# Mixture-of-experts tail of a transformer layer: nine full tiles last, added straight into the output

## The reference

```python
xn = layernorm(h)
gates = softmax(xn @ Wg + bg)                 # 8 experts
g = gates * top_2_mask; g = g / sum(|g|)
y_e = gelu(xn @ W1[e] + b1[e]) @ W2[e] + b2[e]   # 256 -> 1024 -> 256
out = h + sum over the token's two experts of g_e * y_e
```

## Time and profile before

| what | value |
|---|---|
| time, median of 3 runs (lowest, highest) | 585.12 us (585.07, 585.44) |
| time of the profiled execution | 583.82 us |
| its span in the profile | 582.0 us |
| PE busy | 521.7 us, 90% of the span |
| DVE, ACT, POOL busy | 235.3, 267.6, 200.6 us |
| mean load of the 16 DMA engines, last two of 40 slices | 1 and 4 tenths |
| bytes moved | 78.55 MB |

### The profile page before, as it was taken

The page is one execution under the profiler, slowest core; times in us unless marked ns, Lnnn a source line. Parts: engine busy times, 40 slices in busy tenths (PEclk is TensorE's granted clock), DMA queues, the critical chain, the costliest instruction groups (busy, mean ns, idle before and its releaser), DMA issues.

```text
span 582.0 us, 13228 instructions
## 1 busy us (share of the span) xinstructions
PE 521.7 (90%) x3742; PEld 427.2 (73%) x3743; DVE 235.3 (40%) x1083; ACT 267.6 (46%) x1003; POOL 200.6 (34%) x186
## 2 busy tenths in 40 slices
PE   4799889899889988986899999999999999999990
PEld 3466555566556655644899989999999999999970
DVE  2677677777658756644112411111111111111110
ACT  1267677778667766844334332333333333333310
POOL 3132133224443344361133355333333333333221
PEclk9899999999889988985999999999999999999995
DMA  8890020212030303037556565666666666666614
GB/s 264 270 294 2 19 92 20 93 36 92 2 91 18 91 19 92 18 102 255 169 150 170 160 173 176 182 181 182 180 181 181 181 180 181 181 181 182 180 25 153
DMA packets 50999, 78.55 MB, mean 135 GB/s; under 512 B 10528, under 2 KB 39472, under 8 KB 50768
## 3 DMA queue, kind: packets, MB, share of 16 engines
q1 hardware_dynamic: 40160, 66.80, 35.5%
q0 software_dynamic: 8592, 10.58, 10.8%
q10 hardware_dynamic: 2208, 0.71, 0.6%
HBM read 68.27 MB, written 11.90 MB: 138 GB/s over the span
## 4 chain that ended last, share of the span: by engine, by line
PE 50%; issue 28%; POOL 9%; DMA 4%; DVE 3%; another core or an unknown queue 2%; ACT 2%; POOLq 0%; SPq 0%; DVEq 0%; ACTq 0%
PE psVO L972 21%; PE psS L960 12%; PE psP L960 11%; POOL kbd L259 4%; DMA fold<-xn_dram,sel 2%; POOL rstd L424 2%; POOL meta_dram L433 2%; PE psQK L790 2%; PE psQK L948 2%; ACT prob L587 1%; DMA sel<-meta_dram 1%; PE psP L823 1%; DVE prob L1138 1%; DMA sum_dram<-fold,sel 1%
## 5 line engine op out<-in xcount | busy, mean ns | idle before, releaser
L972 PE MATMUL psVO<-xw,prob 128*128 x624 | 141.6, 380 | 0.8 <-DVE fold L1359 0.8
L972 PEld LDWEIGHTS psVO<-xw,prob 128*128 128x128 f32 x624 | 115.6, 190 | 15.5 <-issue 1.2
L487 POOL DMA_INDIRECT sum_dram<-fold,sel x39 | 61.7, 1582 | 167.3 <-DMA sel<-meta_dram 123.5
L587 ACT ACTIVATE prob<-prob,smin 128x128 f32<-128x128 f32 x256 | 99.5, 394 | 10.4 <-DVE smin L1138 8.1
L680 ACT ACTIVATE prob<-psS,b1T 128x128 f32<-128x128 f32 x160 | 45.5, 368 | 98.1 <-PE psS L960 93.0
L424 POOL TENSOR_TENSOR rstd<-ve,minus_half 128x1 f32<-128x1 f32 x32 | 29.0, 906 | 165.1 <-DVE ve L1101 165.1
L680 ACT ACTIVATE prob<-psP,b1T 128x128 f32<-128x128 f32 x152 | 43.2, 373 | 85.5 <-PE psP L960 81.6
L960 PEld LDWEIGHTS psS<-fold,w1c 128*128 128x128 f32 x640 | 77.0, 198 | 1.9 <-DVE fold L1354 1.0
L960 PE MATMUL psS<-fold,w1c 128*128 128x128 f32 x640 | 77.6, 281 | 0.6 <-DVE fold L1354 0.6
L960 PEld LDWEIGHTS psP<-fold,w1c 128*128 128x128 f32 x608 | 70.7, 192 | 3.0 <-DVE fold L1354 2.1
L960 PE MATMUL psP<-fold,w1c 128*128 128x128 f32 x608 | 71.1, 275 | 1.9 <-DVE fold L1354 1.9
(11 more groups left out here) (165 smaller groups left out, 542.9 us busy)
## 6 DMA issues: line engine op xcount, KB each, us to landing
w1c<-in_L_ffn_W SPq DMA_DIRECT2D x39, 1024.0 KB
xw<-in_x SPq DMA_DIRECT2D x16, 512.0 KB, 7.2
xw<-in_L_ffn_W SPq DMA_DIRECT2D x8, 1024.0 KB
sum_dram<-h_all SPq DMA_DIRECT2D x17, 128.0 KB
xn_dram<-xn SPq DMA_DIRECT2D x16, 128.0 KB
out<-sum_dram SPq DMA_DIRECT2D x4, 512.0 KB, 5.7
relb<-in_L_ffn_b SPq DMA_DIRECT2D x1, 1024.0 KB, 4.7
sel<-meta_dram SPq DMA_DIRECT2D x39, 2.0 KB
```

What stands on the lines that cost most here:

```text
L487: pool.indirect_dma_start(out=sum_dram.ap()[0:EARLY_B * S if j < EARLY else N_TOK + P, :], out_offset=bass.IndirectOffsetOnAxis(ap=row_no[ ...
L587: i = act.activation(blk, blk, ACT.Exp, bias=smin[:, k:k + 1], scale=-1.0, accum_out=ssum[:, k:k + 1])
L972: i = pe.matmul(psVO[:, 0:D], hT[u][:, c * P:(c + 1) * P], xw2[:, bass.ds(e * (HC * D) + c * D, D)], start=(c == 0), stop=(c == HC - 1))
```

## The change

- The experts' full tiles of all sixteen images are at least 25, so nine more than the sixteen early ones are certainly full (`LAST` = 9). They are worked on last, as tiles 30 to 38. The `MID` = 14 tiles between (16 to 29) hold the rest, among them all tiles that are partly filled or unused.
- When the scatter of tile 29 has landed, SP copies `sum_dram` to `out` by the same four DMAs, between the loads for tile 33 and those for tile 34. POOL waits for these copies (`fin_out`) before the scatter of tile 30, and scatters 30 to 38 add to `out`. The copies at the end are gone.
- POOL's order from tile 33 on is `gather(33)`, `gather(34)`, `scatter(30)`, then `gather(j)`, `scatter(j-4)`. So four scatters instead of three stand behind the last pair of a gather and a scatter.
- `yout` has two buffers. DVE waits for the scatter of tile j-2 to land, and POOL for that of tile j-1 before it issues scatter j.
- The tables are made in three pieces. The late counts come between result 5 and `xs_evac(8)`, the table of the middle tiles between result 6 and `xs_evac(9)`, that of the last tiles between result 7 and `xs_evac(10)`; `tables_ok` then counts to 3. Two operations per table that were not waited for are now.

```diff
-LATE = TILES - EARLY
+LAST = -(-(SLOTS - E * (P - 1)) // P) - EARLY
+MID = TILES - EARLY - LAST
+TABLE = max(EARLY, MID, LAST)
...
-        yout = fold[:, 3 * D:4 * D]
+        yout = [fold[:, 3 * D:4 * D], sel[:, 0:D]]
...
-            sp.wait_ge(tables_ok, 2)
+            sp.wait_ge(tables_ok, 3)
             sp.wait_ge(scat, 16 * TOPK * B)
             next_records(EARLY)
             load_w1(EARLY - 1, 1)
-            with sp.Fori(EARLY // 2, TILES // 2) as t:
+            with sp.Fori(EARLY // 2, (EARLY + MID) // 2 + 2) as t:
+                for u in range(2):
+                    next_records(2 * t + (u + 1))
+                    load_w1(2 * t + u, u)
+            out_v = out.rearrange("b p d -> (b p) d")
+            rows_ = N_TOK // 4
+            sp.wait_ge(y_scat, 16 * (EARLY + MID))
+            for i in range(4):
+                sp.dma_start(out_v[i * rows_:(i + 1) * rows_, :],
+                             sum_dram.ap()[i * rows_:(i + 1) * rows_, :]).then_inc(fin_out, 16)
+            with sp.Fori((EARLY + MID) // 2 + 2, TILES // 2) as t:
                 for u in range(2):
                     next_records(2 * t + (u + 1))
                     load_w1(2 * t + u, u)
             load_w1(TILES - 1, 0)
+            sp.wait_ge(fin_out, 16 * 4)
             sp.wait_ge(y_scat, 16 * TILES)
-            out_v = out.rearrange("b p d -> (b p) d")
-            rows_ = N_TOK // 4
-            for i in range(4):
-                sp.dma_start(out_v[i * rows_:(i + 1) * rows_, :],
-                             sum_dram.ap()[i * rows_:(i + 1) * rows_, :]).then_inc(fin_out, 16)
-            sp.wait_ge(fin_out, 16 * 4)
...
             def scatter(j):
                 pool.wait_ge(y_sb, j + 2)
+                if j > 0:
+                    pool.wait_ge(y_scat, 16 * j)
+                if j == EARLY + MID:
+                    pool.wait_ge(fin_out, 16 * 4)
                 own_wait(pool)
                 pool.indirect_dma_start(
-                    out=sum_dram.ap()[0:EARLY_B * S if j < EARLY else N_TOK + P, :],
+                    out=sum_dram.ap()[0:EARLY_B * S if j < EARLY else N_TOK + P, :] if j < EARLY + MID
+                    else out.rearrange("b p d -> (b p) d"),
                     out_offset=bass.IndirectOffsetOnAxis(ap=row_no[:, j * META + 2:j * META + 3], axis=0),
-                    in_=yout, in_offset=None, compute_op=ALU.add).then_inc(y_scat, 16)
+                    in_=yout[j % 2], in_offset=None, compute_op=ALU.add).then_inc(y_scat, 16)
...
                 gather(j)
-                scatter(j - 3)
+                if j < EARLY + MID + 3:
+                    scatter(j - 3)
+                elif j > EARLY + MID + 3:
+                    scatter(j - 4)
...
-            for j in range(TILES - 3, TILES):
+            for j in range(TILES - 4, TILES):
                 scatter(j)
...
+            def early_tables():
+                tile_counts(c_t[:, :], 0)
+                tile_table(0, EARLY, c_t[:, :])
+                dve.sem_inc(tables_ok, 1)
+            def late_counts():
+                tile_counts(c_t[:, :], 0)
+                then(dve.tensor_tensor(c_t[:, :], c_t[:, :], taken[:, 0:E], ALU.subtract))
+                tile_ends(c_t[:, :])
+                tiles_taken(c_last, c_t[:, :], LAST)
+                then(dve.tensor_tensor(taken_too[:, 0:E], taken[:, 0:E], c_last, ALU.add))
+                tile_counts(c_all, P - 1)
+                then(dve.tensor_tensor(c_all, c_all, taken_too[:, 0:E], ALU.subtract))
+            def middle_table():
+                tile_table(EARLY, MID, c_all, taken_too)
+                dve.sem_inc(tables_ok, 1)
+            def last_table():
+                tile_table(EARLY + MID, LAST, c_last, taken)
+                dve.sem_inc(tables_ok, 1)
...
-                if not (isinstance(j, int) and j == 0):
-                    dve.wait_ge(y_scat, 16 * j)
-                dve.tensor_scalar(yout, ysum, metas[:, bass.ds(j * META + 1, 1)], None, ALU.mult) \
+                if not (isinstance(j, int) and j <= 1):
+                    dve.wait_ge(y_scat, 16 * (j - 1))
+                dve.tensor_scalar(yout[u], ysum, metas[:, bass.ds(j * META + 1, 1)], None, ALU.mult) \
                     .then_inc(y_sb, 1)
```

More of the change, by code:

```diff
@@ L168, in vit_layer_kernel @@
         row_no = metas.bitcast(I32)
[L169 to L173, removed]
+        at = 1280
+        c_ge, c_gt = (fold[0:1, at + i * TABLE * E:at + (i + 1) * TABLE * E] for i in range(2))
+        at += 2 * TABLE * E
+        c_w, incl = (fold[0:1, at + i * E * E:at + (i + 1) * E * E] for i in range(2))
+        at += 2 * E * E
+        c_e, c_off, c_in, tile_no = (fold[0:1, at + i * TABLE:at + (i + 1) * TABLE] for i in range(4))
+        at += 4 * TABLE
+        c_step, c_room, c_all, c_last, taken_step = (fold[0:1, at + i * E:at + (i + 1) * E] for i in range(5))
+        at += 5 * E
+        taken, taken_too = (fold[0:1, at + i * (E + 1):at + (i + 1) * (E + 1)] for i in range(2))
         psS = [ps("psS0"), ps("psS1")]
@@ L1326, in tile_table @@
                 then(dve.tensor_tensor(c_in[:, 0:tiles], tile_no[:, 0:tiles], c_off[:, 0:tiles], ALU.add))
-                if late:
-                    then(dve.tensor_scalar(c_in[:, 0:tiles], c_in[:, 0:tiles], taken[:, 0:1], float(E * ROW_TILES),
+                if first is not None:
+                    then(dve.tensor_scalar(c_in[:, 0:tiles], c_in[:, 0:tiles], first[:, 0:1], float(E * ROW_TILES),
                                            ALU.add, ALU.min))
-                dve.tensor_scalar(tile_row[:, at:at + tiles], c_in[:, 0:tiles], float(P), None, ALU.mult) \
-                    .then_inc(tables_ok, 1)
@@ L1333, in tiles_taken @@
[L1333 to L1338 removed]
+                then(dve.tensor_scalar(tile_row[:, at:at + tiles], c_in[:, 0:tiles], float(P), None, ALU.mult))
@@ new lines, in tiles_taken @@
+            def tiles_taken(dst, src, tiles):
+                then(dve.tensor_tensor(c_room[:, :], src, c_end[:, :], ALU.subtract))
+                then(dve.tensor_scalar(c_room[:, :], c_room[:, :], float(tiles), 0.0, ALU.add, ALU.max))
+                then(dve.tensor_tensor(dst, c_room[:, :], src, ALU.min))
+            def early_tables():
[10 more added lines that the diff above has]
+                then(dve.tensor_tensor(c_all, c_all, taken_too[:, 0:E], ALU.subtract))
@@ L1378, in _ @@
             xs_evac(2)
-            result(0, expert(0))
+            result(0, 0, expert(0))
             xs_evac(3)
-            result(1, expert(1))
+            result(1, 1, expert(1))
             xs_evac(4)
-            result(2, expert(2))
+            result(2, 0, expert(2))
             keep_logits(B - 1)
@@ L1389, in _ @@
             masks(B // NG - 1)
-            result(3, expert(3))
+            result(3, 1, expert(3))
             xs_evac(6)
             gates(B // NG - 1)
-            result(4, expert(4))
+            result(4, 0, expert(4))
             rows(B // NG - 1)
             xs_evac(7)
-            result(5, expert(5))
-            tile_table(EARLY, LATE, P - 1, True)
-            dve.wait_ge(tables_ok, 2)
+            result(5, 1, expert(5))
+            late_counts()
             xs_evac(8)
-            result(6, expert(6))
-            with dve.Fori(8, TILES - 1) as j:
-                xs_evac(j + 1)
-                result(j - 1, expert(j - 1))
-            for j in range(TILES - 2, TILES):
-                result(j, expert(j))
+            result(6, 0, expert(6))
+            middle_table()
+            xs_evac(9)
+            result(7, 1, expert(7))
+            last_table()
+            dve.wait_ge(tables_ok, 3)
+            xs_evac(10)
+            result(8, 0, expert(8))
+            xs_evac(11)
+            with dve.Fori(5, TILES // 2 - 1) as t:
+                for u in range(2):
+                    result(2 * t + (u - 1), 1 - u, expert(2 * t + (u - 1)))
+                    xs_evac(2 * t + (u + 2))
+            result(TILES - 4, 1, expert(TILES - 4))
+            xs_evac(TILES - 1)
+            for j in range(TILES - 3, TILES):
+                result(j, j % 2, expert(j))
 _INS = ['x', 'L0_tok_w1', 'L0_tok_b1', 'L0_tok_w2', 'L0_tok_b2', 'L0_attn_Wq', 'L0_attn_Wk', 'L0_attn_Wv',
```

38 lines of the change are left out of this document (18 added, 20 removed).

## The result

| | before | after |
|---|---|---|
| median of 5 runs (lowest, highest) | 585.44 us (585.07, 586.60) | 582.30 us (581.76, 582.45) |
| profiled execution, its span | 583.82, 582.0 us | 581.76, 580.0 us |

The ratio is 0.9935, with a 95% interval of 0.9908 to 0.9962. The change gains 3.1 us where 8.3 were predicted, and the time lies above the predicted range.

The account below looks back on a forecast made before the run. PE alone was taken to set the pace in the middle of the expert stage, with copies and scatters behind it at the end. Terms: -9.0 - 0.37 + 0.4 + 0.5 + 0.2 = -8.27 us, giving 576.8 us; range 575.5 to 579.8.

Parts of the forecast that it names:

- The copies leave the end: End of the kernel: without the final copies, all but what follows a landing is saved, 9.0 us gained.
- Rival 3: End of the kernel: it doesn't shorten, as something else ends as late as the copies; 585.3 us, chance 0.02.
- Two buffers: Last tile: DVE's product need not wait for `yout`, so the last scatter leaves 0.37 us earlier.
- Real rows: Last scatters: rows spread over `out` land later than neighbouring ones, 0.4 us lost (0 to 0.94).
- The copies in the middle: Tile 34: load or gather delayed by the copies makes PE wait, 0.5 us lost (0 to 4.4).
- The term for `W1`: Tile 34's load behind the copies: done at 526.2, wanted at 526.19, a wait of 0 to some tenths.
- POOL has caught up by scatter 36: Scatters behind the copies: each needs 3.65 us of a 7.24 us period, so the lag of four costs nothing.
- Tables: Table making: one more step before gather 0 loses 0.2 us (0.05 to 0.4); the late table's pieces cost 0.
- rival 4: Tile 34 and last scatters: everything covered, no wait or slower scatters; 575.95 us, or 575.6 with free tables; chance 0.20.

Follow-up runs that it names:

- e0_before_again: The kernel before, unchanged, in a single execution: 572.58 us.
- h2_before_lag4: The kernel before with one edit, scatter(j-4) instead of scatter(j-3) behind gather(j): 582.20 us, ratio to before 0.9961.
- f0_after_again: The changed kernel, unchanged, timed again on another chip: 566.17 us, ratio to before 0.9897.
- h0_after_third: The changed kernel, unchanged, timed once more as base line of its chip: 582.58 us, ratio to before 0.9953.
- f1_no_copies: The changed kernel without its four copies in the middle and the waits for them: 567.90 us, ratio to before 0.9928.
- e1_end_wait: The changed kernel with POOL waiting for the last scatter's landing before it leaves its block: 570.13 us.
- e2_dve_entry: The changed kernel with DVE's loop turned by half a tile, entered before the copy of tile 11's rows: 569.05 us, ratio to before 0.9957.
- e3_lag4: The changed kernel with scatter(j-4) behind every gather from tile 4 on: 566.49 us, ratio to before 0.9897.
- f2_lag4_then5: The changed kernel with scatter(j-4) up to tile 33, gather 35 ahead of scatter 30, then scatter(j-5): 566.60 us, ratio to before 0.9905.
- h1_records_first: f2_lag4_then5 with, besides, the records of tile 35 loaded ahead of the copies: 582.37 us, ratio to before 0.9959.
- f3_no_last_scatters: The changed kernel without the scatters of tiles 37 and 38, a single execution: 558.49 us.

## Why the prediction was wrong, point by point

From the last sum to the end of the span the prediction had -8.97 us (-9.0 - 0.37 + 0.4); it was 14.98 us and became 10.42, so -4.56. Up to the last sum it had +0.7 us; that sum came 2.53 us later. These two differences, 4.4 and 1.8 us, are the whole miss in the profiled executions, where 2.0 us of the span were gained.

This table is worked out from each trace: what tile 8's to tile 38's first product takes beyond 30 periods of 7.2425 us, then from the last sum to the last scatter's issue, and from there to the end.

```
kernel              PE late, us   sum to scatter   scatter to end
before              1.81          1.98             13.00
e0_before_again     2.86          2.14             13.54
h2_before_lag4      0.07          1.94             13.68
after               2.76          1.71              8.71
f0_after_again      5.43          3.58              8.71
h0_after_third      4.32          3.67              8.71
f1_no_copies        2.55          1.70              8.71
e1_end_wait         1.88          1.71             11.17
e2_dve_entry        1.79          1.68              8.71
e3_lag4             2.08          1.68              8.75
f2_lag4_then5       1.07          3.36              8.75
h1_records_first    1.57          3.89              8.75
```

f3_no_last_scatters, whose end is another, has 4.44 us in the first column. The traces of f0_after_again and h0_after_third are of slow executions, 3.6 and 4.6 us above their medians.

**The copies leave the end: -9.0 predicted.** This is the step that failed most. It said that "what follows a landing stays (582.0 - 581.6 = 0.4)". Measured: from scatter to end 13.00 us became 8.71, so 4.3 gained, and 4.9 us follow the landing. Shown by f3_no_last_scatters and e1_end_wait. From the trace of before the bound could have been worked out: POOL's closing step ended at 577.51, so taking all copies away could bring the end no further than 577.7. Rival 3 was of the right kind, something else that ends late, though not as late as the copies, and it was excluded by a wrong reading: "every engine is idle" is said of busy time, and this instruction counts as none.

**Two buffers: -0.37.** 1.98 became 1.71 us, -0.27, where POOL is not behind. The forecast is right in kind. Where the scatters have piled up, the step is 3.4 to 3.9 us instead, and the buffer is worth nothing.

**Real rows: +0.4 (0 to 0.94).** Scatters 37 and 38 landed after 3.83 and 3.78 us, before 3.65 and 3.62. That is 0.17 us each; and since POOL's DRAIN does not wait for the landing, that of the last costs nothing.

**The copies in the middle: +0.5, at tile 34.** The place was wrong. At PE they cost nothing in the lag that the change has, and gather 34 had left before them (it landed after 4.46 us), so a gather that stands beside all of them, which the prediction reckons with, did not occur. The term for `W1` was near: in the three changed kernels with the longer lag, where no gather from tile 9 to 33 had made PE late, it waited 0.7 to 1.2 us for that load. The load for tile 33, which the prediction read as done by 515.4, had its last landing at 516.17; nothing hangs on it. What the copies do hold up is scatter 30, and what fails then is the sentence "POOL has caught up by scatter 36". It took 3.65 us for each scatter, but one that leaves just before a load of `W1` needs more. All scatters of tiles 9 to 29 in the thirteen traces, by how long before the next load's issue they leave (a landing is the last mark of the DMA's semaphore; where marks are missing from a trace it can be some tenths later):

```
issued before the load by   number   landing after (least, median, most), us
under 1.3 us                22       5.59  6.55  7.77
1.3 to 1.5 us                8       4.52  5.12  5.52
1.5 to 2.4 us              241       3.33  3.85  4.63
just behind the last load    2       4.81        5.25
```

The eight of the second row are all of tile 9. It is not the tile that counts: the scatters of tiles 26 to 29 landed after 3.7 to 3.8 us in f0_after_again, where they left 1.5 us or more ahead of the load, and after 5.25 to 7.43 us in the four kernels with the longer lag, where they left less than 1.3 us ahead, or just behind the last one. No run moved one scatter alone, so that the time of its issue is the cause is read from these groups and not shown by an edit.

That would also explain why the state lasts: with 6.6 us to land and 0.8 to the next issue a scatter takes 7.4 us, more than a tile's 7.24, so the next one leaves late too and again falls in with a load. In the trace of the first result this went on from tile 9 to 15, and it is what made gather 18 leave late: it stood behind scatter 14, which waited for scatter 13 (6.30 us). In the kernels with the longer lag it begins at tile 26; why there, no run shows. By the Trainium skill (DMA: Bandwidth & Descriptors, Queues, rings and completion order) an engine takes the queues in turn. That alone does not give these landings: 21 of the 22 late scatters landed after the load of 1 MB that was issued behind them, by 0.7 us in the median, and the load itself landed after 4.8 to 6.2 us; the scatters that left 1.3 us or more ahead of a load had landed at least 1.8 us before it. So a late scatter comes 2.7 us later than one that leaves early, and no earlier than the load. What on the engines holds it is open. In the first trace the pile was gone by scatter 37, as it was in e1 and e2; in f0_after_again and h0_after_third it was not, and cost 1.9 and 2.0 us (3.58 and 3.67 against 1.71), and there DVE, waiting for a buffer, also kept PE at tile 38 (periods of 7.99 and 7.80 us).

**Tables: +0.2.** From the table's first operation to SP's step it took 2.89 us (262.91 to 265.80) instead of 2.72 (261.90 to 264.62), 0.17 us longer, and no piece of the late one kept PE waiting (the copy of tile 10's rows was done 2.4 us before PE needed them). Right. In rival 4 the time without a cost of the tables is 585.12 - 9.37 = 575.75, not 575.6; that changes nothing.

**What was not counted: late gathers.** Between tiles 8 and 38 PE lost 1.81 us in before and 2.76 in after in the first pair of traces, 2.86 in the other trace of before, 5.43 and 4.32 in the two others of after; h2_before_lag4 shows 0.07. How much of the difference between before and after is the change and how much the execution stays open: with the same lag other traces of changed kernels show 1.79, 1.88, 2.55 and 4.44. For the first pair the account closes so: 4.3 + 0.3 gained at the end; lost 0.74 in the first images, 0.6 from there to tile 0 (0.17 of it the table), 0.2 in tiles 0 to 8 and 0.95 behind them, together 2.5; 2.1 us of net gain, as the profiled executions have it (583.82 and 581.76; 582.02 and 579.99 in the spans). The medians have 3.1 us; the 0.74 us in the first images at least is no matter of the change.

None of the versions is shown to be faster than the changed kernel. What they point to, a longer lead for the gathers and a shorter chain behind the copies at once, was not found, and no version was tried in which POOL is done before the last tiles and the output is still whole.

## What to carry to other kernels

Before taking work off the end of a kernel, ask for every engine what its own closing takes, instructions without busy time included: an engine that had been done "long ago" may be what ends next. Where PE is 100% busy in a window, list for each load and gather the time from issue to need against the time to land; a lead of 6.7 us against landings of up to 7.5 (median 5.9 for the gathers of tiles 9 to 33) is a loss waiting to happen, and moving one issue ahead is cheap. And when transfers must follow one another, count the catching-up with the landing that they have just before a load, not with that on idle engines.

## What was unexpected of the hardware

- The closing instruction of POOL takes 6.8 to 7.0 us from its last operation in all thirteen traces, with or without DMAs still on their way.
- A scatter of 128 rows lands after 3.85 us when it leaves 1.5 us or more before a load of 1 MB, and after 6.55 us (both medians) when it leaves less than 1.3 us before it; then it lands after the load.
- The same kernel has a median of 571.5 us on one chip and of 585 on another. In two traces of before, from the first product of tile 0 to the end they agree (309.5 and 308.3 us); the difference of 12 us arises ahead of it. TensorE's granted clock from 150 to 200 and 200 to 230 us is 1.00 on the faster chip and 0.94 and 0.91 on the slower. That this is the cause is not shown; the mean over the span doesn't tell the chips apart (0.969 for 570.8 us, but 0.968 for the 580.0 us of after).
